# A one-core AdaLN block with routed experts: the down product as three half-precision terms

## Chip, core and metric

The kernel runs on 1 core of one Trainium2 chip. The metric is device time in microseconds (us) of one execution. The engines are named as the profile names them: PE (TensorE matmuls), PEld (its weight loads), DVE (VectorE), ACT (ScalarE), POOL (GpSimd), SP (SyncE, which issues most DMAs). "PE's queue" below is the order in which PE takes its instructions; every engine takes its own in order.

## What is computed

1024 tokens (4 batches of 256) with 256 features go through a modulated layer norm, a linear attention with a residual, a second modulated layer norm, a router that picks 2 of 8 experts for each token, and the experts. The part that the change touches is the experts:

```python
for e in range(8):
    gate = silu(xt @ Wg[e].T)                # 256 -> 704
    up = xt @ Wu[e].T                        # 256 -> 704
    out = out + gate * up @ Wd[e].T * comb[:, e:e + 1]   # 704 -> 256
```

## The kernel before

**Two parts.** The first 120 us are the front: ten steps `k = 0..9` of a software pipeline over the four batches (the attention, the second norm, the router's logits), then the routing (`routing_choice`, `routing_places`, `routing_table`), which sorts 2048 token-expert pairs into 23 tiles of 128 slots, each tile with one expert. The second part is `tile_step` for tiles 0 to 22.

**In the front** batch b is at stage `at_step(k, n)` when b = k - n. On ACT, stage 1 reads Q out of PSUM (L678) and lets PE compute the attention sums (L489) and then the attention output (L501); stage 2 turns the sums into weights (L686, L694); stage 5 copies h2T (L704), and the router's matmuls follow (L533). On DVE, stage 3 adds the attention output (L993) and stage 4 normalises (L998 to L1018). Between these stages the same queues carry the preparation of the experts' first-layer weights W1.

**Preparation of W1 for expert e** splits its float32 matrices in a high and a low f16 half under one power-of-two scale: SP loads both matrices in a staging buffer (L354; two buffers, each free again when `low` of its expert is done); ACT squares them with a running sum (`sum_squares`, L638); PE adds the sums over partitions (`norm`, L414, two matmuls of 2 columns each); DVE makes the scale (`power_scale`, L862 to L865); ACT writes the high halves (`high`, L646, four instructions of 704 columns); DVE writes the low halves (`low`, L873, four of 704). Experts 0 to 3 are prepared in the steps, 4 and 5 around the routing, 6 and 7 in tiles 1 to 6. W2 (the down matrix) is loaded in float32 and used as it is.

**A tile c** on PE: `gate_up(c)` (18 f16 matmuls: 3 terms, 2 chunks, 3 pieces; L572), `turn_slots(c+1)` (2 transposes, L561), `down(c-1)` (6 float32 products, each recorded as 2 matmuls of 256 columns; L600), `turn_act(c)` (6 transposes, L584). For c < 8, `gate_up(c)` waits until W1 of expert c is split, whatever expert the tile has. ACT makes the silu of each piece (L723), copies the next tile's rows to f16 (L717) and copies a third of the turned activations (L733, L734); DVE multiplies (L1043), makes the low half of the rows and the slot's factors (L1032 to L1037), scales the result (L1052) and copies the other two thirds (L1067). POOL scatters the result and gathers rows by indirect DMA (L1142, L1128).

## Time and profile before

| | us |
|---|---|
| three runs | 319.64, 319.98, 322.03 |
| median | 319.98 |
| the profiled execution's own time | 321.41 |
| its span, first to last instruction | 319.57 |
| mean granted TensorE clock | 0.873 of full |

Times below are in us from the start of the span. A line such as L572 is a line of the kernel. "[1.35 <-X]" behind an instruction is how long its engine sat idle before it and what ended that. In the chain of waits each piece follows from the one before it. PEclk in the table of windows is the granted share of TensorE's clock; 1.00 is 2.4 GHz and 0.50 is 1.2 GHz.

### The profile page before, as it was taken

What the parts mean: (1) busy time and instruction counts of PE and PEld (TensorE: products, weight loads), DVE (VectorE), ACT (ScalarE), POOL (GpSimd) and SP (SyncE); (2) the same over time, 40 slices, a digit from 0 to 9 for tenths busy, and PEclk for the clock granted to TensorE, in tenths of its full rate; (3) what the DMA queues carried; (4) which work ended last, traced back from release to release, by engine and by line L of the source; (5) the groups of instructions that cost most, each with busy time, mean ns of one, the idle gap of its engine ahead of it and who ended that gap; (6) DMA issues with size and microseconds to landing.
All of it is one profiled execution on the core that took longest, in us unless ns stands there. A gap on an engine that the chain in (4) does not pass through costs nothing.

```text
span 319.6 us, 4248 instructions
## 1 busy us (share of the span) xinstructions
PE 248.6 (78%) x1154; PEld 157.7 (49%) x1155; DVE 170.7 (53%) x448; ACT 119.7 (37%) x262; POOL 82.5 (26%) x93
## 2 busy tenths in 40 slices
PE   3889298967452228999997899999999999999500
PEld 0236166656352113666664466666666666666300
DVE  1356805798877972844667244444444444443236
ACT  1158367427828243564453222223232323222000
POOL 0103646531100051022242122223333222211223
PEclk9999859997555556999999799999999999999955
DMA  7993270418072925231011111011010111100083
GB/s 266 362 417 127 71 295 33 180 25 352 2 257 105 301 69 207 91 126 29 33 36 33 33 33 35 21 36 33 17 45 29 33 34 44 33 2 0 0 269 125
DMA packets 12663, 33.88 MB, mean 106 GB/s; under 512 B 2049, under 2 KB 7684, under 8 KB 11624
## 3 DMA queue, kind: packets, MB, share of 16 engines
q1 hardware_dynamic: 10152, 28.51, 24.5%
q0 software_dynamic: 2208, 5.17, 5.5%
q8 instruction: 8, 0.13, 0.2%
q10 hardware_dynamic: 288, 0.02, 0.1%
q14 instruction: 7, 0.06, 0.1%
HBM read 29.45 MB, written 5.14 MB: 108 GB/s over the span
## 4 chain that ended last, share of the span: by engine, by line
PE 68%; DVE 18%; DMA 5%; ACT 4%; issue 3%; SPq 1%; POOL 0%; DVEq 0%; POOLq 0%; ACTq 0%
PE bank L572 27%; PE bank L600 19%; PE bank L584 5%; PE bank L464 4%; PE bank L501 2%; DVE W L873 2%; ACT W L646 2%; PE bank L421 2%; DMA W<-expert_parts 2%; PE bank L477 2%; PE bank L561 2%; DMA x<-in_x 2%; PE bank L489 1%; DMA rows<-token_rows,source_i 1%; PE bank L533 1%
## 5 line engine op out<-in xcount | busy, mean ns | idle before, releaser
L572 PE MATMUL bank<-W,rows 128*128 x414 | 90.2, 374 | 4.2 <-DVE W L873 3.2
L600 PE MATMUL bank<-W,shared 128*128 (+1 forms) x276 | 67.9, 388 | 0.7 <-DVE shared L1067 0.7
L572 PEld LDWEIGHTS bank<-W,rows 128*128 128x128 f16 x414 | 41.6, 101 | 46.8 <-issue 10.4
L1043 DVE SCALAR_TENSOR_TENSOR shared<-bank,unscale,rows 128x256 f32<-128x256 f32 (+1 forms) x69 | 31.7, 461 | 60.7 <-ACT rows L723 56.2
L1142 POOL DMA_INDIRECT expert_parts<-shared,dest_i x23 | 23.3, 1014 | 131.4 <-DVE shared L1052 131.4
L600 PEld LDWEIGHTS bank<-W,shared 128*128 128x128 f32 (+1 forms) x276 | 48.7, 189 | 13.4 <-issue 8.6
L723 ACT ACTIVATE rows<-bank,unscale 128x256 f32<-128x256 f32 (+1 forms) x69 | 31.4, 455 | 51.8 <-PE bank L572 40.9
L1128 POOL DMA_INDIRECT rows<-token_rows,source_i x23 | 25.7, 1118 | 34.9 <-DVE source_i L843 28.2
L646 ACT ACTIVATE W<-staged,w_scale_bits 128x704 f16<-128x704 f32 x32 | 25.9, 870 | 11.7 <-DVE w_scale_bits L863 11.7
L733 ACT ACTIVATE shared<-bank 128x128 f32<-128x128 f32 x23 | 6.4, 277 | 62.1 <-PE bank L584 62.1
L873 DVE SCALAR_TENSOR_TENSOR W<-staged,w_scale_bits,W 128x704 f16<-128x704 f32 x32 | 29.4, 966 | 0.0
L1052 DVE TENSOR_SCALAR shared<-bank,slot_weight 128x256 f32<-128x256 f32 x23 | 11.1, 484 | 27.9 <-PE bank L600 27.9
L638 ACT ACTIVATE W<-staged 128x1408 bf16<-128x1408 f32 x16 | 21.8, 1368 | 5.3 <-DMA staged<-in_w 5.3
L584 PE MATMUL bank<-keep,shared 128*128 128x128 f32 x138 | 20.0, 281 | 1.2 <-DVE rows L1032 1.2
L584 PEld LDWEIGHTS bank<-keep,shared 128*128 128x128 f32 x138 | 14.2, 137 | 8.0 <-issue 6.6
L464 PE MATMUL bank<-W 128*128 128x512 f32 x32 | 16.8, 674 | 0.8 <-DVE gate_bias L940 0.8
L1067 DVE COPY shared<-bank 128x512 f32<-128x512 f32 x23 | 15.9, 690 | 1.3
L421 PE MATMUL bank<-W,condT 128*4 128x512 f32 x12 | 9.6, 968 | 5.4 <-ACT condT L630 5.4
L561 PE MATMUL bank<-keep,rows 128*128 128x128 f32 x46 | 9.1, 280 | 5.5 <-DMA rows<-token_rows,source_i 5.5
L489 PE MATMUL bank<-kinv,rows 128*128 128x1 f32 x32 | 4.9, 274 | 8.1 <-ACT shared L678 7.7
L477 PE MATMUL bank<-W 128*128 128x256 f32 x48 | 11.2, 382 | 0.0
L464 PEld LDWEIGHTS bank<-W 128*128 128x128 f32 x32 | 6.8, 222 | 8.2 <-issue 8.2
(155 smaller groups left out, 255.6 us busy)
## 6 DMA issues: line engine op xcount, KB each, us to landing
staged<-in_w SPq DMA_DIRECT2D x8, 1408.0 KB, 6.4
W<-in_w SPq DMA_DIRECT2D x8, 768.0 KB, 8.8
W<-expert_parts SPq DMA_DIRECT2D x8, 256.0 KB, 4.8
W<-in_wmod SPq DMA_DIRECT2D x3, 512.0 KB, 7.4
token_rows<-rows SPq DMA_DIRECT2D x1, 1040.0 KB, 5.8
x<-in_x SPq DMA_DIRECT2D x4, 256.0 KB, 8.8
W<-mod_rows SPq DMA_DIRECT2D x4, 256.0 KB, 4.4
out<-x SPq DMA_DIRECT2D x4, 256.0 KB, 2.3
```

The costliest lines, as they stand in the source:

```text
L464: mm = pe.matmul(bank[3 + t][:, :], hT[:, col:col + P], v3(w_inT, DC)[:, dc, D:3 * D], start=(dc == 0), stop=(dc == DC - 1))
L477: mm = pe.matmul(bank[bk][:, c:c + S], v3(w_inT, DC)[:, dc, w0:w0 + P], hT[:, dc * TOKENS + b * S:dc * TOKENS + (b + 1) * S], start=(dc == ...
L572: mm = pe.matmul(bank[2 + n][:, 0:2 * w], slot[:, kc * P:(kc + 1) * P], W1_pairs[:, bass.ds(e * 2 + part, 1), :, kc, n * PIECE:n * PIECE + w],
L584: mm = pe.transpose(bk[0:rows, col:col + P], act[:, fc * P:fc * P + rows], keep[:, C_ID:C_ID + P])
L600: mm = pe.matmul(bank[7][:, 0:D], actT[0:rows, fc * P:(fc + 1) * P], W2[0:rows, bass.ds(e * W2_EXP + fc * D, D)], start=(fc == 0), stop=(f ...
L638: sc.activation(W1_b16[:, at:at + W1_MAT], staged[e % STAGED][:, m * W1_MAT:(m + 1) * W1_MAT], ACT.Square, accum_out=sumsq[:, 2 * e + m:2 ...
L646: sc.activation(w1_part(e, 0, m, kc), staged[e % STAGED][:, at:at + F], ACT.Identity, scale=w_scale[:, 2 * e + m:2 * e + m + 1]).then_inc( ...
L723: sc.activation(sig[:, n * PIECE:n * PIECE + w], bank[2 + n][:, 0:w], ACT.Silu, scale=unscale[c % 2][:, 0:1]).then_inc(s["sig_ok"], 1)
L873: ve.scalar_tensor_tensor(w1_part(e, 1, m, kc), staged[e % STAGED][:, at:at + F], w_scale[:, 2 * e + m:2 * e + m + 1], w1_part(e, 0, m, kc ...
L1043: ve.scalar_tensor_tensor(act[:, n * PIECE:n * PIECE + w], bank[2 + n][:, w:2 * w], unscale[c % 2][:, 1:2], sig[:, n * PIECE:n * PIECE + w ...
L1128: po.indirect_dma_start(xs[j % 4], None, rows_d, bass.IndirectOffsetOnAxis(source_i[:, j:j + 1], 0), bounds_check=last_token, oob_is_err=F ...
L1142: po.indirect_dma_start(parts_d, bass.IndirectOffsetOnAxis(dest_i[:, j:j + 1], 0), y_sb[r], None, bounds_check=last_part, oob_is_err=False ...
```

## The change

W2 and the activations are split in high and low f16 halves as W1 and the rows are, and the down product becomes 18 f16 matmuls of 256 columns (high x high, high x low, low x high). What goes with it:

- **W2 is prepared**: per expert one unit of 1536 columns: squares with a running sum (ACT), a `norm` matmul of one column (PE), `power_scale` (DVE), `high` in two instructions of 768 columns (ACT), `low` in two of 768 (DVE; for experts 5, 6 and 7 on POOL, two instructions for each half, after the scatters of tiles 1, 4 and 6).
- **W1's scale** comes from the largest neuron's norm: the squares are written without a running sum, PE adds them up in 8 matmuls of 352 columns with bf16 ones (before: 2 of 2 columns), and `power_scale` begins with a reduction over 352 columns.
- **Staging** is by unit (one matrix), in five smaller buffers; each load waits for `low` of the unit five before it.
- **Where it stands**: the tables below name step or tile and (expert, W1 or W2).
- **Tile**: ACT writes the high half of the turned activations (512 and 256 columns), DVE subtracts for the low half (512 and 256), in place of the copies; the last chunk of the activations overlaps the one before it, so that all transposes and products have 128 rows. DVE gets one small instruction more for the slot's weight.

```diff
+        SQUARES_AT = {0: (0, W1_OF), 1: (1, W1_OF), 3: (0, W2_OF), 4: (1, W2_OF), 5: (2, W1_OF), 6: (3, W1_OF),
+                      7: (2, W2_OF), 8: (3, W2_OF), 9: (4, W1_OF)}
+        NORM_AT = {1: (0, W1_OF), 2: (1, W1_OF), 4: (0, W2_OF), 5: (1, W2_OF), 6: (2, W1_OF), 7: (3, W1_OF), 8: (2, W2_OF)}
+        HIGH_AT = {2: (0, W1_OF), 3: (1, W1_OF), 4: (0, W2_OF), 5: (1, W2_OF), 6: (2, W1_OF), 7: (3, W1_OF), 8: (2, W2_OF)}
+        LOW_AT = {3: (0, W1_OF), 4: (1, W1_OF), 5: (0, W2_OF), 6: (1, W2_OF), 7: (2, W1_OF), 8: (3, W1_OF), 9: (2, W2_OF)}
+        TILE_SQUARES = {0: [(5, W1_OF)], 1: [(5, W2_OF)], 4: [(6, W2_OF)], 6: [(7, W2_OF)]}
+        TILE_SQUARES_END = {2: [(6, W1_OF)], 4: [(7, W1_OF)]}
+        TILE_NORM = {1: [(5, W1_OF)], 2: [(5, W2_OF)], 3: [(6, W1_OF)], 5: [(6, W2_OF), (7, W1_OF)], 7: [(7, W2_OF)]}
+        TILE_HIGH = {1: [(5, 0)], 2: [(5, 2)], 3: [(6, 0)], 5: [(6, 2), (7, 0)], 7: [(7, 2)]}
+        TILE_HIGH_END = {1: [(5, 1)], 3: [(6, 1)], 5: [(7, 1)]}
+        TILE_LOW = {0: [(4, 2)], 2: [(5, 1)], 4: [(6, 1)], 6: [(7, 1)]}
+        TILE_LOW_END = {1: [(5, 0)], 3: [(6, 0)], 5: [(7, 0)]}
+        POOL_LOW = {1: [(5, 2)], 4: [(6, 2)], 6: [(7, 2)]}
...
+            def norm(e, of):
...
+                    for k in range(count):
+                        mm = pe.matmul(bank[n % 2][:, 0:FOLD], ones16[:], parts[:, k, :], start=(k == 0), stop=(k == count - 1))
...
@@ down
-                for fc in range(FC):
-                    rows = min(P, F - fc * P)
-                    mm = pe.matmul(bank[7][:, 0:D], actT[0:rows, fc * P:(fc + 1) * P],
-                                   W2[0:rows, bass.ds(e * W2_EXP + fc * D, D)],
-                                   start=(fc == 0), stop=(fc == FC - 1))
+                terms = [(a, fc, part) for a, part in ((act_hi, 0), (act_hi, 1), (act_lo, 0)) for fc in range(FC)]
+                for k, (a, fc, part) in enumerate(terms):
+                    mm = pe.matmul(bank[7][:, 0:D], a[:, fc * P:(fc + 1) * P],
+                                   W2_16[:, bass.ds(e * 2 * W2_EXP + part * W2_EXP + fc * D, D)],
+                                   start=(k == 0), stop=(k == len(terms) - 1))
...
@@ scalar, the steps (highs stands where high stood: before the read of Q)
-                if k in (2, 3, 6, 7):
-                    high({2: 0, 3: 1, 6: 2, 7: 3}[k], 0)
+                if k in HIGH_AT:
+                    highs(HIGH_AT[k], 0)
                 for b in at_step(k, 1):
                     sc.wait_ge(s["q_done"], b + 1)
...
@@ scalar, the tile, behind the silus and slots_out
+                for prep in at_tile(TILE_SQUARES, i, c):
+                    squares(*prep)
+                for unit in at_tile(TILE_HIGH, i, c):
+                    high(*unit)
+                sc.wait_ge(s["at_done"], 2 * (4 * i + c) + 1)
+                sc.activation(act_hi[:, 0:4 * P], bank[5][:], ACT.Copy).then_inc(s["act_hi_ok"], 1)
                 sc.wait_ge(s["at_done"], 2 * (4 * i + c) + 2)
+                sc.activation(act_hi[:, 4 * P:6 * P], bank[6][:, 0:2 * P], ACT.Copy).then_inc(s["act_hi_ok"], 1)
...
@@ vector, after the steps
+            power_scale(3, W2_OF)
             routing_choice(ve, link)
-            power_scale(4)
+            power_scale(4, W1_OF)
             routing_places(ve, link)
+            power_scale(4, W2_OF)
             routing_table(ve, link)
-            power_scale(5)
+            low(3, 2)
             low(4, 0)
             low(4, 1)
...
@@ gpsimd, for W2 of experts 5, 6 and 7
+                for h, cols in enumerate(halves(e, m)):
+                    po.wait_ge(s["hi_ok"], 2 * n + h + 1)
+                    klink(po.tensor_scalar(staged[n % STAGED][:, cols], staged[n % STAGED][:, cols], scale_of(e, m), None, ALU.mult))
+                    po.tensor_tensor(unit_out(W1_16, W2_16, e, m, 1)[:, cols], staged[n % STAGED][:, cols],
+                                     unit_out(W1_16, W2_16, e, m, 0)[:, cols], ALU.subtract).then_inc(s["pool_lo_ok"], 1)
```

In a step, `power_scale` stands on DVE behind the read of Q (L964, L966) and ahead of L993; PE's `norm` stands ahead of the Q product for k < 5 and behind the transposes of L524 for k >= 5; ACT's squares close a step. PE's `norm(3, W2)` follows the steps, `norm(4, W1)` and `norm(4, W2)` the counting matmuls (L545). In a tile, PE's `norm` stands between `down(c-1)` and `turn_act(c)`, DVE's `power_scale` between the result (L1052) and the activations. `down(c)` for c < 8 waits until W2 of expert c is split. ACT after the steps does the exponential, then `high` of (3, W2), (4, W1), the squares and `high` of (4, W2).

## Rows read from the trace of the kernel before

**Rows 1.** The page's first part: busy time, share, instructions of each engine

```profile
span 319.6 us, 4248 instructions
PE 248.6 (78%) x1154; PEld 157.7 (49%) x1155; DVE 170.7 (53%) x448; ACT 119.7 (37%) x262; POOL 82.5 (26%) x93
```

**Rows 2.** Windows: length, each engine's busy us (instructions), PEclk, DMA share, GB/s

```profile
71.50:82.90 11.40, 7.61 (x34) 6.06 (x34) 9.67 (x27) 9.54 (x14) 1.71 (x2) 0.65 0.61 255
82.90:94.50 11.60, 6.79 (x30) 6.51 (x30) 9.20 (x22) 4.37 (x7) 0.86 (x1) 0.50 0.40 137
94.50:120.40 25.90, 6.44 (x30) 4.32 (x29) 21.00 (x90) 13.77 (x19) 4.47 (x4) 0.50 0.51 168
120.40:177.00 56.60, 52.30 (x258) 32.17 (x258) 32.57 (x74) 27.15 (x59) 13.89 (x13) 0.95 0.22 79
177.00:237.00 60.00, 59.97 (x298) 37.70 (x298) 24.78 (x62) 16.14 (x46) 14.42 (x15) 0.97 0.10 30
```

**Rows 3.** Chain of waits, start of tiles 0, 9 and a late one: start, us, what

```profile
120.38 6.44 PE bank L572 x18
...
193.63 3.57 PE bank L572 x18
...
237.89 3.57 PE bank L572 x18
241.67 2.79 PE bank L600 x12
244.46 0.81 PE bank L584 x6
245.26 3.56 PE bank L572 x18
```

**Rows 4.** Groups by form: count | busy us, mean ns | idle before

```profile
L572 PEld LDWEIGHTS bank<-W,rows 128*128 128x128 f16 x414 | 41.6, 101 | 46.8 <-issue 10.4
L638 ACT ACTIVATE W<-staged 128x1408 bf16<-128x1408 f32 x16 | 21.8, 1368 | 5.3 <-DMA staged<-in_w 5.3
L822 DVE TENSOR_REDUCE slot_tile<-shared 128x16 f32<-128x384 f32 x1 | 0.6, 554 | 0.0
L704 ACT ACTIVATE W<-bank 128x512 f32<-128x512 f32 x4 | 2.3, 585 | 8.2 <-PE bank L533 4.4 <-PE bank L524 3.8
L1113 POOL TENSOR_TENSOR rows<-W 128x512 f32<-128x512 f32 x4 | 5.4, 1352 | 0.3
L1116 POOL TENSOR_SCALAR ksq_max<-ksq 128x2 f32<-128x2 f32 x4 | 0.9, 213 | 0.0
```

**Rows 5.** Instructions in time, ACT and DVE, steps 6 and 8: start, us

```profile
76.46 3.20 ACT L646 ACTIVATE W<-staged,w_scale_bits 128x704 f16<-128x704 f32 x4 [1.82 <-DVE w_scale_bits L863]
89.12 3.54 DVE L873 SCALAR_TENSOR_TENSOR W<-staged,w_scale_bits,W 128x704 f16<-128x704 f32 x4
```

**Rows 6.** Chain of waits, steps 4 to 6

```profile
60.97 0.48 ACT shared L678
...
62.72 1.85 PE bank L501 x8
...
70.58 0.80 DVE W L993 x2
71.52 3.52 PE bank L501 x8
```

**Rows 7.** Chain of waits, end of the steps and counting

```profile
92.63 1.89 PE bank L533 x8
94.54 0.67 DVE lg L756 x4
...
100.51 0.43 PE bank L414 x2
```

**Rows 8.** Instructions in time around the gate of tile 7

```profile
173.00 0.87 PE L584 MATMUL bank<-keep,shared 128*128 128x128 f32 x6
177.03 3.58 PE L572 MATMUL bank<-W,rows 128*128 x8 [3.16 <-DVE W L873]
```

More of the change, by code:

```diff
@@ L55 @@
 C_COLS = C_LOW + P
+W1_OF, W2_OF = 0, 1
+PREPARED = [(0, W1_OF), (1, W1_OF), (0, W2_OF), (1, W2_OF), (2, W1_OF), (3, W1_OF), (2, W2_OF), (3, W2_OF),
+            (4, W1_OF), (4, W2_OF), (5, W1_OF), (5, W2_OF), (6, W1_OF), (6, W2_OF), (7, W1_OF), (7, W2_OF)]
+UNITS = [(e, m) for e, of in PREPARED for m in ((0, 1) if of == W1_OF else (2,))]
+NTH = {prep: n for n, prep in enumerate(PREPARED)}
+UNIT = {unit: n for n, unit in enumerate(UNITS)}
+UNIT_COLS = max(W1_MAT, W2_EXP)
 S_BIN, S_BSWAP, S_BOUT = 0, 6, 7
@@ L97, in laid_out @@
     turned = [np.concatenate([by_partition(np.ascontiguousarray(m[e].T)) for m in (Wg, Wu)], axis=1) for e in range(E)]
[L98 to L99 removed]
+    gap = np.zeros((FC * P - F, D), np.float32)
+    at = (FC - 1) * P
+    down = [by_partition(np.concatenate([Wd[e].T[:at], gap, Wd[e].T[at:]], axis=0)) for e in range(E)]
     w_in_t = np.concatenate([W_in.T, W_in[:P][pairs].T], axis=1)
@@ L258, in small_col, with unit_out, halves, units_of @@
             return small[:, c:c + 1]
-        def w1_part(e, part, m, kc):
-            at = (2 * e + part) * W1_EXP + m * W1_MAT + kc * F
-            return W1_16[:, at:at + F]
+        def unit_out(buf1, buf2, e, m, part):
+            if m == 2:
+                at = (2 * e + part) * W2_EXP
+                return buf2[:, at:at + W2_EXP]
+            at = (2 * e + part) * W1_EXP + m * W1_MAT
+            return buf1[:, at:at + W1_MAT]
+        def halves(e, m):
+            w = (W2_EXP if m == 2 else W1_MAT) // 2
+            return [slice(h * w, (h + 1) * w) for h in range(2)]
+        def units_of(e, of):
+            return [(e, 0), (e, 1)] if of == W1_OF else [(e, 2)]
+        def scale_of(e, m):
+            c = 4 * e + (3 if m == 2 else 1)
+            return w_scale[:, c:c + 1]
         W1_pairs = W1_16.rearrange("p (x m c f) -> p x m c f", m=2, c=DC, f=F)
@@ L466, in _ @@
                         mm.then_inc(s["kv_done"], 1)
-                if k in (1, 2):
-                    norm(k - 1)
+                if k in NORM_AT and k < 5:
+                    norm(*NORM_AT[k])
                 for b in at_step(k, 1):
@@ L526, in _ @@
                     mm.then_inc(s["th_done"], 1)
-                if k in (6, 7):
-                    norm(k - 4)
+                if k in NORM_AT and k >= 5:
+                    norm(*NORM_AT[k])
                 for b in at_step(k, 6):
@@ L615, in tile_step @@
                     down(i, c - 1)
-                if isinstance(i, int) and i == 0 and c in NORM_TILES:
-                    norm(NORM_TILES[c])
+                for prep in at_tile(TILE_NORM, i, c):
+                    norm(*prep)
                 turn_act(i, c)
@@ new lines, in low, with lows @@
+                for h, cols in enumerate(halves(e, m)):
+                    ve.wait_ge(s["hi_ok"], 2 * n + h + 1)
+                    ve.scalar_tensor_tensor(unit_out(W1_16, W2_16, e, m, 1)[:, cols], staged[n % STAGED][:, cols], scale_of(e, m),
+                                            unit_out(W1_16, W2_16, e, m, 0)[:, cols], ALU.mult, ALU.subtract).then_inc(s["lo_ok"], 1)
+            def lows(prep, turn):
+                units = units_of(*prep)
+                for e, m in units[turn:turn + 1]:
+                    low(e, m)
@@ L1055, in tile_step @@
             def tile_step(i, c):
-                first = isinstance(i, int) and i == 0
                 mult_pieces(i, c)
@@ L1145, in _ @@
                     gather(j + 4)
+                for unit in POOL_LOW.get(j, []):
+                    low(*unit)
             po.wait_ge(s["gateb_in"], 16 * B)
```

306 lines of the change are left out of this document (172 added, 134 removed).

## The prediction

> **What bounds the kernel now.** I read the page's totals first. PE is busy for 78% of the span, but no other engine is idle enough to ignore [rows 1]. The windows then split the span. In tiles 8 to 15 PE is busy 59.97 of 60.00 us at the full clock, so PE alone sets the pace there, while DVE and ACT have more than half their time free [rows 2]. In the steps and the routing it is different. From 71.5 to 94.5 PE is busy for 14.4 of 23.0 us and DVE for 18.9, and in the routing DVE has 21.0 of 25.9 us, with TensorE at half clock [rows 2]. The chain of waits there alternates between DVE, PE and ACT [rows 6, 7]. A microsecond taken off PE is thus worth a microsecond in the tiles, and one put on ACT, DVE or PE's queue in the front costs up to its full length. The change takes from the first and puts on the second.
>
> **The gain per tile.** The chain of one late tile is 3.57 (gate and up), about 0.2 (two transposes), 2.79 (down), 0.81 (six transposes); the next tile's gate and up start 7.37 after this one's [rows 3]. The gate and up matmuls stream 3 terms x 2 chunks x 1408 columns = 8448 columns in 3.57 us, 0.423 ns a column. A down matmul in f16 has 256 columns: 0.108 us, if its weight load (101 ns [rows 4]) lies under the one before, as the loads of L572 do. 18 x 0.108 = 1.95 us in place of 2.79: 0.84, with the last chunk now at full height. I take 0.85 a tile, so a period of 6.5. From above: pairs that don't overlap would take 18 x (0.101 + 0.108) = 3.76 us.
>
> What ran beside `down` must still fit. Per tile ACT loses two copies and gets 512 and 256 columns, about 0.6 + 0.4 (585 ns for 512 [rows 4]); DVE gets about 0.7 + 0.4 in place of its copy, and one small instruction more. ACT is then busy near 2.8 and DVE near 4.1 (3.3 before) of 6.5 us (from 16.1 and 24.8 us in 60 [rows 2]). Late tiles stay bound by PE. The high and low activations are ready some 1.6 us into the next gate and up, which lasts 3.57, so `down` doesn't wait. For 23 tiles that is 19.6 us, if nothing else happened.
>
> **The preparation in the front.** Prices: a W2 unit costs ACT squares of 1536 columns, 1.37 x 1536/1408 = 1.5 us [rows 4], and `high` of 2 x 768 columns at 0.80 per 704, 1.75 us [rows 5]; `low` costs DVE 2 x 0.885 x 768/704 = 1.95 us [rows 5]; its scale 0.5 plus one dependent instruction, 0.65. The W1 `norm` streams 8 x 352 = 2816 columns: 1.2 us at full clock, 2.4 at half; before it was 0.43 at half clock [rows 7]. The new reduction over 352 columns: 554 x 352/384 = 0.5 us [rows 4]. Now place by place, as the delay it adds to the chain:
>
> - Steps 1 and 2: two reductions and the longer `norm`, some 1.5 us on DVE's chain. Part of it is taken back, because PE then starts the K and V products nearer to its return to full clock. I take 0, from above 1.5.
> - Step 4: ACT's `high(0, W2)` stands before the read of Q (L678), but its scale is made by DVE in the same step behind DVE's own read of Q. Before, ACT read Q at 60.97 [rows 6]. Now DVE reads Q (0.8), makes the scale (0.35), then ACT writes 1.75 us and only then reads Q, near 64.0: **3.0**. PE's sums and y(1) (62.72) wait for that.
> - Step 5: DVE runs `low(0, W2)` (1.95) and the scale (0.65) ahead of L993, which stood at 70.58 right behind the normalisation: 2.6. ACT again has `high(1, W2)` (1.75) ahead of the sums and weights of the last batch, so that PE's y(3) (71.52 before) waits for ACT: 1.6 more. Together **4.2**.
> - Steps 6 and 7: PE's `norm` of (2, W1) and (3, W1) at half clock, 2.4 - 0.45, and the reduction 0.5, each directly ahead of what DVE does next: **2.5 + 2.4**. `low(1, W2)` lies under y(3), 3.52 us of PE at half clock [rows 6]; without it, 1.95 more.
> - Step 8: `high(2, W2)` ahead of the last h2T copy: **1.1**.
> - Step 9: `low(2, W2)` and the scale of (3, W2) on DVE ahead of the logits (94.54 [rows 7]). 2.6, of which DVE waited about 1.4 anyway: **1.2**.
> - Routing: `norm(4, W1)` in place of 0.43 [rows 7] at half clock 2.0, reduction 0.5, one dependent multiply and a copy 0.3, the scale of (4, W2) ahead of `routing_table` 0.65: **3.4**.
> - `low(3, W2)` ahead of `low(4, ...)` fits under the first gather, less 0.2.
>
> Sum 18.0: tile 0 should start near 138.4, not 120.4.
>
> **The preparation in the tiles.** Tiles 0 to 8 took 73.25 us from the start of tile 0 (120.38) to that of tile 9 (193.63) [rows 3]; the gate of expert 7 cost about 5 of it, PE idle for 3.16 us on DVE's `low` and then slow [rows 8]. Now they are 9 x 6.5 = 58.7, and on top: half clock in tile 0, 2.9; `norm`s between `down` and `turn_act`, 3 x 1.2 + 3 x 0.3 = 4.5. In tiles 2 and 4 the second half of `high` W1 stands on ACT ahead of the next silus: 1.2 and 1.9. In tiles 3 and 6 `high` waits for a scale which DVE makes behind its own `low` and result; the activations' high half waits behind it, DVE's low half behind that, and the next `turn_slots` and `down` behind that: 2.8 and 4.2. Last, W2 of expert 7: its `high` ends about 1.5 us into tile 8 and POOL then has four instructions of 768 columns before `down(7)`, due 3.8 us into the tile. A two-input POOL instruction costs 1352 ns per 512 columns [rows 4], 2.0 us for 768. For the one-input kind there is only 213 ns for 2 columns [rows 4]; bounds 0.2 and 2.0, I take 1.3. 2 x 3.3 = 6.6, behind POOL's two DMA issues: `down(7)` waits about 5.0 (3 to 7). These sum to 22.5, so 81.2 us: **8.0 longer**. The preparation of experts 5 to 7 is 3 x 9 us of ACT, and with ACT's own 2.8 a tile it fills some 49 of 52 us, so little slack is left to absorb an order that is wrong.
>
> The Trainium skill (GPSIMD Engine Reference, Engine selection) has one-input work on POOL at about line rate and two-input work about twice as slow as on VectorE. By it the one-input instruction would be an estimated 0.9 us and the wait some 0.8 us shorter; no row here shows it.
>
> **The sum.** 319.6 + 18.0 + 8.0 - 14 x 0.85 (tiles 9 to 22, 11.9) = 333.7 us of span. The profiled execution's own time is 321.41 and its span 319.57; the median of the runs is 319.98, 0.4 above the span. So I forecast 334.
>
> **Rivals.**
>
> - *The preparation hides* (faster). If ACT and DVE ran the W2 units in their idle stretches, only `norm` and reductions would remain (about 8 in the front) and tiles 0 to 8 would not lose: 319.6 + 8 - 19.6 + 0 to 4, near 310. For it: over the span ACT is busy 37% and DVE 53% [rows 1]. Against it: engines take their queues in order, and steps 4 and 5 have the scale behind the read on DVE and `high` ahead of the read on ACT. It decides if front and tiles 0 to 8 together add less than 11.9. Chance 0.06.
> - *Half of it hides* (within 1%): the front adds 8 and tiles 0 to 8 add 4, so 320. This needs PE at full clock through steps 6 to 9, against the windows' 0.50 to 0.65 [rows 2]. Chance 0.05.
> - *More is lost*: POOL slower than 2 us an instruction under DVE's traffic, a half-clock stretch after each stall (the gate of tile 7 cost one: eight matmuls of L572 took 3.58 there, and usually eighteen do [rows 3, 8]), steps 1 and 2 in full: 334 + 3 + 4 + 1.5, beyond 343. Chance 0.07.
> - *The loads don't hide at 256 columns*: 3.76 - 2.79 = 0.97 more a tile in place of 0.85 less, 23 x 1.82 = 42 us above the forecast, 376. Against it: the same loads hide wholly under L572's matmuls, where 18 x (101 ns + the matmuls' columns) would be 5.4 us, not 3.57 [rows 3, 4]. Chance 0.02. The Trainium skill (TensorE: Matmul & The Clock Gate, "The mechanism" of Part 3) says LDWEIGHTS overlaps matmuls in flight only if the row group differs. By that rule full-height loads wouldn't overlap; the trace disagrees with it for 512 columns.
> - The forecast: 0.80.
>
> **Range and chances.** Low: steps 6 to 9 and the routing at full clock (-4), POOL's short price (-2), a stall or two in tiles 3 and 6 absorbed (-3): 325. High: 343 as above. The cases below 325 hold 0.11 and those above 343 0.09, so 325 to 343 leaves out 2 in 10. A measurement of this kernel tells about 1% from no change. Faster by over 1%: 0.06; within 1%: 0.05; slower: 0.89.
>
> **What would show it.** After: the late tiles' gate and up start 6.5 us apart and the 18 down matmuls take 1.95; if 3.8, the loads don't hide. ACT's read of Q (L678's successor) for batch 3 comes about 3 us after PE's Q product ends, with ACT's idle time before it released by DVE's scale. PE idles about 4 us ahead of y(3). The bf16 `norm` takes 2.4 us at half clock in steps 6 and 7. Tile 0 starts 14 to 20 us later than 120.4; if it starts within 10, the queue argument is wrong. PE idles once for about 5 us ahead of `down(7)`, released by POOL. If the end is early although all of these show, the tiles' stalls were counted twice.

## The result, and the profile after

The changed kernel takes 344.87 us (median of four, 343.43 to 346.44) against 319.85 for the kernel before (319.64 to 322.03): a ratio of 1.077, 95% interval 1.070 to 1.084. It is slower by 25 us; the forecast was 14 slower, 334 (325 to 343), so the median lies 1.9 above the range. Timed again beside the later experiments the changed kernel took 343.01 (339.52 to 345.44), ratio 1.066 (1.059 to 1.073), which is the upper end of the range. The profile of that second run ("the changed kernel again") has a span of 341.2 us and is the one that I compare experiments with. Its code is the same.

The page's first part for the kernel after, to be read against [rows 1]:

```profile
span 344.6 us, 4994 instructions
PE 247.2 (72%) x1356; PEld 160.9 (47%) x1357; DVE 202.5 (59%) x548; ACT 151.4 (44%) x278; POOL 105.0 (30%) x105
```

PE is busy for as long as before: `down` takes some 19 us less (an estimate, 23 tiles of 0.82), and the longer norms and stretches at half clock take that up again. DVE and ACT are busy for 32 us more each, and the span grew by 25 us in which PE is idle. Line numbers from here on are those of the changed kernel: gate and up is L629, `down` L656, `turn_act` L641, the W1 `norm` L468, `high` L707, DVE's `low` L957, POOL's `low` L1241 and L1242, the read of Q L745, the attention sums L545 with ACT's weights L761, y L557.

Windows of the kernel after: length, busy us (instructions) of PE, PEld, DVE, ACT, POOL, granted clock, DMA share, GB/s. They are y(3) to the logits, the routing with the first gather, tiles 0 to 8, and 60 us of late tiles:

```profile
82.10:112.50 30.40, 18.57 (x80) 14.94 (x80) 23.07 (x58) 19.78 (x24) 2.56 (x3) 0.61 0.39 126
112.50:142.10 29.60, 8.48 (x34) 4.85 (x35) 23.62 (x97) 10.76 (x14) 4.95 (x4) 0.50 0.33 100
142.10:231.00 88.90, 72.43 (x409) 43.43 (x410) 50.79 (x127) 47.34 (x84) 38.67 (x28) 0.86 0.25 83
240.00:300.00 60.00, 60.00 (x414) 41.46 (x412) 34.47 (x93) 23.81 (x57) 18.86 (x19) 1.00 0.13 39
```

Before, the stretches that answer to the first two rows took 23.0 and 25.9 us [rows 2]. The third is where the forecast failed: tiles 0 to 8 took 73.25 us before [rows 3], they were forecast at 81.2 and take 88.9, with PE at 0.86 of its clock and idle for 16 us. The last row is the gain, with PE never idle at the full clock. A late tile in the chain of waits (start, us, what):

```profile
237.86 3.56 PE bank L629 x18
241.43 0.22 PE bank L618 x2
241.65 1.97 PE bank L656 x18
243.61 0.66 PE bank L641 x6
244.27 3.56 PE bank L629 x18
```

Eighteen down matmuls take 1.97 us (1.95 forecast) where twelve took 2.79 [rows 3], and the period is 6.40 us.

Where the rest went, by starting times in the two traces:

| start of | before | forecast | changed, again | miss |
|---|---|---|---|---|
| first z (step 3) | 54.9 | 54.9 | 54.9 | 0 |
| second z (behind step 4) | 64.6 | +3.0 | 70.2, +5.6 | 2.6 |
| y(3) (behind step 5) | 71.5 | +7.2 | 81.2, +9.7 | 2.5 |
| fourth z (step 6) | 76.5 | +9.7 | 88.2, +11.7 | 2.0 |
| x2 of batch 3 (step 7) | 84.0 | +12.1 | 97.9, +13.9 | 1.8 |
| logits (step 9) | 94.5 | +14.4 | 110.6, +16.1 | 1.7 |
| tile 0 | 120.4 | +18.0 | 140.3, +19.9 | 1.9 |
| tile 9 | 193.6 | +26.0 | 227.8, +34.2 | 8.2 |
| end | 319.6 | +14.1 | 341.2, +21.6 | 7.5 |

In the first profile tile 0 came at 142.1 and tiles 0 to 8 took 88.9; in this one 140.3 and 87.5.

### The profile page after: what moved, and what is told of

Its sections match the earlier page's. It is cut to its first block, busy times and chain, and to the rows that moved or that the text cites. A ratio compares the mean times of both kernels' runs of the same rounds, so it can differ in the third digit from the quotient of the medians.

```text
span 344.6 us, 4994 instructions
## 1 busy us (share of the span) xinstructions
PE 247.2 (72%) x1356; PEld 160.9 (47%) x1357; DVE 202.5 (59%) x548; ACT 151.4 (44%) x278; POOL 105.0 (30%) x105
## 4 chain that ended last, share of the span: by engine, by line
PE 52%; DVE 22%; ACT 8%; DMA 7%; issue 5%; SPq 3%; POOL 3%; DVEq 0%; ACTq 0%; POOLq 0%
PE bank L629 20%; PE bank L656 13%; DVE W L957 5%; ACT W L707 4%; PE bank L641 3%; DMA staged<-in_w 3%; PE bank L468 3%; PE bank L557 3%; PE bank L520 2%; PE bank L533 2%; DMA W<-expert_parts 2%; DVE shared L1165 1%; PE bank L545 1%; PE bank L618 1%; POOL staged L1241 1%
## 5 line engine op out<-in xcount | busy, mean ns | idle before, releaser
L629 PE MATMUL bank<-W,rows 128*128 x414 | 90.4, 375 | 3.9 <-DVE W L957 2.8
L629 PEld LDWEIGHTS bank<-W,rows 128*128 128x128 f16 x414 | 41.5, 100 | 47.1 <-issue 11.0
L707 ACT ACTIVATE W<-staged,w_scale_bits 128x704 f16<-128x704 f32 (+1 forms) x48 | 40.0, 889 | 50.0 <-DVE w_scale_bits L944 50.0
L656 PE MATMUL bank<-W,shared 128*128 x414 | 53.7, 283 | 10.0 <-POOL W L1242 6.5
L656 PEld LDWEIGHTS bank<-W,shared 128*128 128x128 f16 x414 | 40.9, 100 | 19.3 <-issue 12.0
L957 DVE SCALAR_TENSOR_TENSOR W<-staged,w_scale_bits,W 128x704 f16<-128x704 f32 (+1 forms) x42 | 41.0, 1024 | 0.0
L1165 DVE TENSOR_TENSOR shared<-bank,shared 128x512 f16<-128x512 f32 (+1 forms) x46 | 23.5, 552 | 19.0 <-ACT shared L799 19.0
L799 ACT ACTIVATE shared<-bank 128x512 f16<-128x512 f32 x23 | 13.6, 592 | 40.9 <-PE bank L641 40.9
L699 ACT ACTIVATE W<-staged 128x1408 bf16<-128x1408 f32 x16 | 21.2, 1369 | 4.5 <-DMA staged<-in_w 4.5
L641 PE MATMUL bank<-keep,shared 128*128 128x128 f32 x138 | 19.6, 280 | 2.9 <-DVE rows L1125 2.9
L1150 DVE TENSOR_SCALAR shared<-bank,slot_weight 128x256 f32<-128x256 f32 x23 | 11.1, 483 | 14.1 <-PE bank L656 12.5
L641 PEld LDWEIGHTS bank<-keep,shared 128*128 128x128 f32 x138 | 16.4, 146 | 3.8 <-DVE shared L1140 3.4
L468 PE MATMUL bank<-W,ones 128*128 128x352 bf16 x64 | 14.8, 391 | 2.7 <-ACT W L699 2.7
L557 PE MATMUL bank<-shared,W 128*128 128x256 f32 x32 | 11.5, 521 | 4.1 <-ACT W L761 4.1
L1241 POOL TENSOR_SCALAR staged<-staged,w_scale_bits 128x768 f32<-128x768 f32 x6 | 13.9, 2319 | 0.1
L1221 POOL TENSOR_TENSOR rstd<-var_eps,half_neg 128x2 f32<-128x2 f32 x4 | 3.4, 861 | 32.4 <-DVE var_eps L975 32.4
```

Source lines behind the costliest of these rows:

```text
L468: mm = pe.matmul(bank[n % 2][:, 0:FOLD], ones16[:], parts[:, k, :], start=(k == 0), stop=(k == count - 1))
L629: mm = pe.matmul(bank[2 + n][:, 0:2 * w], slot[:, kc * P:(kc + 1) * P], W1_pairs[:, bass.ds(e * 2 + part, 1), :, kc, n * PIECE:n * PIECE + w],
L641: mm = pe.transpose(bk[:, col:col + P], act[:, at:at + P], keep[:, C_ID:C_ID + P])
L656: mm = pe.matmul(bank[7][:, 0:D], a[:, fc * P:(fc + 1) * P], W2_16[:, bass.ds(e * 2 * W2_EXP + part * W2_EXP + fc * D, D)], start=(k == 0) ...
L707: sc.activation(unit_out(W1_16, W2_16, e, m, 0)[:, cols], staged[n % STAGED][:, cols], ACT.Identity, scale=scale_of(e, m)).then_inc(s["hi_ ...
L957: ve.scalar_tensor_tensor(unit_out(W1_16, W2_16, e, m, 1)[:, cols], staged[n % STAGED][:, cols], scale_of(e, m), unit_out(W1_16, W2_16, e, ...
```

## The stalls in the changed kernel

PE in time, kernel after (start, us, what, idle before it): the sums and y(1) of step 4, y(3) of step 6, then tile 3's `down` and norm, tile 7's gate and up, tile 8's `down` and transposes.

```profile
65.59 1.84 PE L545 MATMUL bank<-kinv,rows 128*128 128x1 f32 x8 [3.57 <-ACT shared L745]
67.28 3.76 PE L557 MATMUL bank<-shared,W 128*128 128x256 f32 x8
...
82.08 3.78 PE L557 MATMUL bank<-shared,W 128*128 128x256 f32 x8 [4.13 <-ACT W L761]
...
172.28 3.26 PE L656 MATMUL bank<-W,shared 128*128 x18 [0.47 <-issue]
175.34 2.18 PE L468 MATMUL bank<-W,ones 128*128 128x352 bf16 x8
...
206.55 5.98 PE L629 MATMUL bank<-W,rows 128*128 x18 [2.77 <-DVE W L957]
...
225.90 4.02 PE L656 MATMUL bank<-W,shared 128*128 x18 [6.45 <-POOL W L1242]
229.71 1.48 PE L641 MATMUL bank<-keep,shared 128*128 128x128 f32 x6
```

ACT in time, same kernel, steps 4 and 5:

```profile
63.21 1.76 ACT L707 ACTIVATE W<-staged,w_scale_bits 128x768 f16<-128x768 f32 x2 [2.74 <-DVE w_scale_bits L944]
...
79.27 1.76 ACT L707 ACTIVATE W<-staged,w_scale_bits 128x768 f16<-128x768 f32 x2 [9.24 <-DVE w_scale_bits L944]
```

The waits are the forecast ones, in the forecast places: `high` stood waiting 2.74 us for DVE's scale with the read of Q behind it, PE waited 3.57 us for that read, y(3) 4.13 us for ACT, `down(7)` 6.45 us for POOL. What was not in the sum stands in the second column, the durations. y(1), eight matmuls that had taken 1.85 us before [rows 6], takes 3.76 behind its stall; `down` in tile 8 takes 4.02 where 1.97 is usual; tile 7's gate and up 5.98 where 3.56 is (5.42 in the second profile, and 5.42 in the kernel before, which has a stall there too). Behind these stalls the granted clock is 0.50 for some microseconds (windows 65.6 to 71.0, 82.1 to 86.0, 206.55 to 209.0 and 225.9 to 229.9). It isn't so behind every one: in tile 6 the six transposes behind 1.72 us of idle time take their usual 0.84, at a granted clock of 1.00. The profile tells nothing yet of whether the half clock costs time or only fills waits, so it was tried.

## The experiments

Two theories run through them. *Q*: an engine takes its queue in order, so W2's preparation costs what stands ahead of the next thing that the attention or the tile needs. *W*: ACT, DVE and PE have more to do and no room for it, wherever it stands. The experiments ran in four groups. The kernel before, timed beside each group, had medians of 319.8 to 321.5 us, so a difference of under 2 us between kernels of two groups is not clear.

### Only `high` of W2 behind the reads of steps 4 and 5

```diff
 # ACT, ahead of the read of Q
-                if k in HIGH_AT:
+                if k in HIGH_AT and k not in (4, 5):
                     highs(HIGH_AT[k], 0)
 # ACT, behind the sums and their weights
-                    highs(HIGH_AT[k], 1)
+                    highs(HIGH_AT[k], 0 if k in (4, 5) else 1)
```

> Only ACT's order in steps 4 and 5 is changed: `high(0, W2)` and `high(1, W2)` stand behind the attention sums and their weights, no longer ahead of the read of Q. The work is the same. Theory Q (an engine takes its queue in order, so what counts is what stands ahead of the attention's next read): the read of Q for batch 3 comes back from 64.9 to about 61.7 us, PE's y(3) waits for ACT 1.8 us less, and tile 0 starts 4.5 us earlier (3 to 6): about 340.4 us. Theory W (ACT, DVE and PE simply have more to do in the front, wherever it stands): tile 0 starts where it did, 344.9 us within 1.

334.45 us (333.83 to 335.32); tile 0 at 131.9 in place of 140.3. This much of the loss is one of order, but the gain of 8.4 to 8.6 us is nearly twice the 4.5 of theory Q. PE in time of this kernel:

```profile
60.65 1.02 PE L545 MATMUL bank<-kinv,rows 128*128 128x1 f32 x8 [0.77 <-ACT shared L745]
61.53 1.97 PE L557 MATMUL bank<-shared,W 128*128 128x256 f32 x8
...
73.02 3.57 PE L557 MATMUL bank<-shared,W 128*128 128x256 f32 x8 [2.04 <-DVE W L1084]
```

The wait fell from 3.57 to 0.77, and the sums and y(1) behind it from 1.84 + 3.76 to 1.02 + 1.97: another 2.6 us that come with the wait. The first z, ahead of the edit, came 1.2 us earlier already (53.7 for 54.9; profiles of one and the same front differ by as much). So 7.2 of tile 0's 8.4 us are the edit's, and 4.5 and 2.6 make 7.1.

### PE kept busy through its waits

In the tiles, with every wait left as it is:

```diff
+        BUSY = {(3, 1): (15, 11), (6, 3): (15, 15), (7, 0): (24, 15), (8, 2): (56, 15)}
...
+                for _ in range(count):
+                    pe.matmul(bank[0][:, 0:D], W2_16[:, 0:P], W2_16[:, 0:D], start=True, stop=True)
```

> The same kernel, with f16 matmuls of 256 columns into an unused bank put where PE stood idle in the tiles: 15 ahead of the slots of tile 3, 15 ahead of the transposes of tile 6, 24 ahead of the gate product of tile 7, 56 ahead of `down(7)`, at about 0.11 us each the length of each idle stretch. Their results are used by nothing. Theory H (half clock behind each stall costs about 7 us in tiles 3, 7 and 8: 2.1 + 2.4 + 2.7): those stretches run at full clock and the time falls by 5.5 us (3 to 7.5): 339.4. Theory S (the stalls are set by ACT, DVE and POOL, and a faster PE only waits longer at the next one): no change, within 1 us. If filling costs more than the idle time holds, the time rises by up to 2 us.

336.87 us (336.76 to 338.06). Its tile 0 came at 140.3 as in the changed kernel again, so the two traces compare directly: tile 3 10.39 in place of 11.92, tile 7 6.59 in place of 8.28, tile 8 13.32 in place of 15.61, tile 9 6.40 in place of 6.71; tile 6 stayed at 12.79, so its filler changed nothing. Together 5.8 us, and theory S is out. PE in time, tiles 6 to 8 of this kernel (L671 are the added matmuls):

```profile
196.74 1.80 PE L671 MATMUL bank<-W 128*128 128x256 f16 x15
...
199.43 2.78 PE L671 MATMUL bank<-W 128*128 128x256 f16 x24
202.37 3.74 PE L631 MATMUL bank<-W,rows 128*128 x18 [0.15 <-issue]
...
212.86 6.28 PE L671 MATMUL bank<-W 128*128 128x256 f16 x56
219.47 2.31 PE L658 MATMUL bank<-W,shared 128*128 x18 [0.34 <-POOL W L1255]
```

The gate product waits just as long for DVE and `down(7)` for POOL as before, but both then run at the full clock (1.00 from 199.4 to 206.0 and from 212.8 to 221.8). Matmuls whose results nobody reads make the kernel 6 us faster. Tile 7's part of it, 1.7 us, is one that the kernel before left lying as well: its tile 7 takes 9.07 us, a late tile 7.38.

In the front, the same in steps 4 to 6 (30, 20 and 34 such matmuls ahead of the sums, the transposes and y(3)):

```diff
+                if k == 4:
+                    keep_busy(30, bank[1], 2)
                 for b in at_step(k, 2):
...
+                if k == 6:
+                    keep_busy(34, bank[0], 3)
                 for b in at_step(k, 3):
...
+                if k == 5:
+                    keep_busy(20, bank[1], 2)
                 for b in at_step(k, 5):
```

> The changed kernel with f16 matmuls of 256 columns into an unused bank in three idle stretches of PE in the front: 30 ahead of the attention sums of step 4 (3.57 us idle), 20 ahead of the transposes of step 5 (2.51), 34 ahead of y(3) in step 6 (4.13). Nothing uses their results; all waits stay. Theory H (a part of what e1 gave back beyond the 4.5 us forecast is TensorE's clock: behind these stalls y(1) took 3.76 us where it took 1.85 before): y(1) and its sums give back 2.6, y(3), its transposes and the norm of step 6 3: 5 us less (3 to 6), about 339 against 344. Theory O (e1's gain is all order: DVE and ACT set the front, a faster PE waits longer): no change within 1.5 us.

338.12 us (337.52 to 340.00) against 343.01 (339.52 to 345.44): 4.9 less in the medians, though the two ranges overlap by 0.5. Tile 0 came at 135.0 in place of 140.3; 1.1 of these 5.3 us stood already at the first z, ahead of the added matmuls. PE in time, this kernel:

```profile
59.77 3.44 PE L476 MATMUL bank<-W 128*128 128x256 f16 x30
63.52 1.02 PE L552 MATMUL bank<-kinv,rows 128*128 128x1 f32 x8 [0.30 <-ACT shared L756]
64.40 1.97 PE L566 MATMUL bank<-shared,W 128*128 128x256 f32 x8
...
77.42 1.99 PE L566 MATMUL bank<-shared,W 128*128 128x256 f32 x8 [0.40 <-ACT W L772]
```

The sums and y(1) are back at 1.02 + 1.97 with the wait still there, and y(3) went from 3.78 to 1.99. Some 4 to 5 us of the front's loss can be had back by the clock alone, with the order left as it is. Before, y(3) took 3.52 at half clock too [rows 6]: a part of this gain is one that the kernel before left lying as well.

### W1's scale from sums as before, W2's preparation whole

```diff
-                        ins = sc.activation(w, staged[n % STAGED][:, 0:W1_MAT], ACT.Square)
+                    ins = sc.activation(w, staged[n % STAGED][:, 0:W2_EXP if m == 2 else W1_MAT], ACT.Square,
+                                        accum_out=sumsq[:, 3 * e + m:3 * e + m + 1])
...
-                        mm = pe.matmul(bank[n % 2][:, 0:FOLD], ones16[:], parts[:, k, :], start=(k == 0), stop=(k == count - 1))
+                        mm = pe.matmul(bank[n % 2][:, 0:1], keep[:, C_ONE:C_ONE + P], sumsq[:, 3 * e + m:3 * e + m + 1],
+                                       start=(m == 0), stop=(m == 1))
...
-                    link(ve.tensor_reduce(norm_sq[:, 0:1], bank[n % 2][:, 0:FOLD], AX.X, ALU.max))
```

> Only W1's scale is made as in the kernel before: ACT's squares sum themselves, `norm` is two one-column matmuls in place of eight of 352 columns, and DVE's reduction over 352 columns is gone. W2's preparation stays whole. Theory Q: steps 1 and 2 give back 1.5, steps 6 and 7 2.4 and 2.0, the routing 2.5, tiles 1, 3 and 5 together 4 (the norms and their half-clock part): about 12 us less, 333 (330 to 337). If the norms hide behind other work: less than 3 us. If W2's squares, `high` and `low` alone carry the loss: no change.

334.62 us (333.43 to 335.09): 8.4 under the changed kernel again and 10.3 under its first timing, where 12 were forecast. Tile 0 came 8.4 us earlier (131.9), tiles 0 to 8 took 85.3 in place of 87.5. The norms by the neurons, which are no part of the f16 product itself, cost more than a third of the whole loss. In the tiles they were partly covered: 2 us, not 4.

### W2's low halves on DVE in place of POOL

```diff
-        TILE_LOW = {0: [(4, 2)], 2: [(5, 1)], 4: [(6, 1)], 6: [(7, 1)]}
-        TILE_LOW_END = {1: [(5, 0)], 3: [(6, 0)], 5: [(7, 0)]}
-        POOL_LOW = {1: [(5, 2)], 4: [(6, 2)], 6: [(7, 2)]}
+        TILE_LOW = {0: [(4, 2)], 2: [(5, 1)], 3: [(5, 2)], 4: [(6, 1)], 6: [(7, 1)]}
+        TILE_LOW_END = {1: [(5, 0)], 3: [(6, 0)], 5: [(6, 2), (7, 0)], 7: [(7, 2)]}
+        POOL_LOW = {}
```

> Only the low halves of W2 of experts 5, 6 and 7 move from POOL to DVE (after tile 3's scales, at the ends of tiles 5 and 7). Theory P (POOL's four instructions of 768 columns are what `down(7)` waited 6.45 us for, and its two-input ones hold DVE up in tiles 4 to 6): the wait ahead of `down(7)` falls to 1 us or less, the half clock behind it (2.7 us) goes too, and of the stall and the slow gate product in tile 7 about half goes: 9 us less, 336 (332 to 339). Theory D (DVE has no room in tiles 3 to 8: 1.95 us more in each of three tiles comes back as waits of the slots and activations): 3 us less or nothing, 342 to 346.

335.46 us (334.79 to 335.88), 7.5 to 9.4 less. PE in time, tiles 7 and 8 of this kernel:

```profile
202.88 6.39 PE L627 MATMUL bank<-W,rows 128*128 x18 [2.04 <-DVE W L955]
...
217.63 2.46 PE L654 MATMUL bank<-W,shared 128*128 x18 [1.45 <-DVE W L955]
```

Tile 8 fell from 15.61 to 8.47 us: 5.0 of that is the wait (6.45 to 1.45) and the rest the clock behind it. That part held. The other did not: the stall ahead of tile 7's gate was 2.04 where it had been 2.77, its product still ran at half clock (6.39), and tiles 6 and 7 took 21.2 where they had taken 21.1. Taking POOL's work away did not help there. Whether POOL had no part in that stall, or DVE's own 1.95 us a unit cost as much in its place, this experiment doesn't tell.

### The same work in another order

In the tiles, with `high` of steps 4 and 5 as in the first experiment: the units stand in the order in which they are due, a `high` one turn behind its norm, one unit on ACT ahead of the activations' copies and one behind them, all low halves on DVE.

```diff
-            (4, W1_OF), (4, W2_OF), (5, W1_OF), (5, W2_OF), (6, W1_OF), (6, W2_OF), (7, W1_OF), (7, W2_OF)]
+            (4, W1_OF), (4, W2_OF), (5, W1_OF), (6, W1_OF), (5, W2_OF), (7, W1_OF), (6, W2_OF), (7, W2_OF)]
...
+        TILE_ACT = {0: [(5, 0, 's'), (5, 1, 's')], 1: [(6, 1, 's'), (5, 2, 's')], 2: [(5, 1, 'h')], 3: [(6, 1, 'h'), (7, 0, 's')],
+                    4: [(5, 2, 'h')], 5: [(7, 1, 'h')], 6: [(6, 2, 'h')], 7: [(7, 2, 'h')]}
+        TILE_ACT_END = {0: [(6, 0, 's')], 1: [(5, 0, 'h')], 2: [(6, 0, 'h')], 3: [(7, 1, 's')], 4: [(7, 0, 'h')], 5: [(6, 2, 's')], 6: [(7, 2, 's')]}
+        TILE_NORM = {1: [(5, W1_OF)], 2: [(6, W1_OF)], 3: [(5, W2_OF)], 4: [(7, W1_OF)]}
+        TILE_NORM_EARLY = {6: [(6, W2_OF)], 7: [(7, W2_OF)]}
```

> The edit of e1_high_after_reads, and another order of the preparation in the tiles, with the same work: the experts' units stand in the order in which they are due (5 and 6 of W1, 5 of W2, 7 of W1, 6 and 7 of W2), ACT makes a `high` one turn after the norm that it needs, about one unit between its slots' copy and its activations' copies and one behind them, and DVE makes all low halves, W2's too. Theory Q (the stalls of tiles 3, 6, 7 and 8 are waits for scales, for `high` and for POOL, not lack of time on ACT or DVE): tiles 0 to 8 take 67 us in place of 87 to 89, so some 20 less than e1: 315 (311 to 320). Theory W (ACT and DVE have no room: DVE has about 57 us of work in them): tiles 0 to 8 stay over 78 us, 326 or more.

314.88 us (314.48 to 316.55): 1.8% under the kernel before, ratio 0.982 (0.973 to 0.992), with all of the change's work in it. Window of this kernel over its tiles 0 to 8, to be read against the third window above:

```profile
133.50:199.80 66.30, 63.69 (x409) 41.47 (x410) 51.39 (x134) 47.79 (x84) 15.11 (x14) 0.97 0.33 111
```

DVE does 51.39 us of work in 66.3 where it did 50.79 in 88.9, ACT 47.79 where it did 47.34. The work is the same and there was room for it: 21 to 23 us were waits, half clock and, on DVE, instructions that POOL made longer (last section). ACT's waits for a scale, by the table of waits, the kernel after first and this kernel second:

```profile
ACT W L707 <- DVE w_scale_bits L944: 50.0, 12, 9.2
```

```profile
ACT W L707 <- DVE w_scale_bits L945: 30.9, 8, 7.0
```

In the front, more of the same on top (ACT's `high` of steps 6 to 8 behind the h2T copy; DVE's scales and lows of steps 5 to 9 between the second norm's differences and h2; expert 4's norms and scales behind the routing table):

```diff
 # DVE, behind the differences
+                if k in NORM_AT and k >= 5:
+                    power_scale(*NORM_AT[k])
...
 # ACT
                     sc.activation(h2T, bank[2][:], ACT.Copy).then_inc(s["h2T_ok"], 1)
+                if k in HIGH_AT and k >= 6:
+                    highs(HIGH_AT[k], 0)
+                    highs(HIGH_AT[k], 1)
...
 # DVE, routing
-            power_scale(4, W1_OF)
             routing_places(ve, link)
-            power_scale(4, W2_OF)
             routing_table(ve, link)
+            power_scale(4, W1_OF)
             low(3, 2)
+            power_scale(4, W2_OF)
```

> e5 and, in the front, more moved behind what the attention needs, with the same work: ACT's `high` of steps 6 to 8 behind the h2T copy, DVE's scales and lows of steps 5 to 9 behind the second norm's differences, the scales and norms of expert 4 behind the routing's table, under the first gather. Theory Q: steps 6 to 9 give back about 4 and the routing 2.5: 6 us less than e5 (3 to 9), about 309. Theory W (half-clock PE and DVE's sheer length set steps 6 to 9, whatever the order): within 2 us of e5.

314.08 us (313.36 to 314.56): 0.8 less, not 6. The fourth z came 4.7 us earlier (76.7 against 81.4) and x2 of batch 3 6.1 earlier (84.9 against 91.0), but h2T of batch 3 0.9 later (100.8 against 99.9). DVE in time of this kernel shows where it was given back:

```profile
92.60 3.54 DVE L961 SCALAR_TENSOR_TENSOR W<-staged,w_scale_bits,W 128x704 f16<-128x704 f32 x4
...
96.05 0.88 DVE L1117 SCALAR_TENSOR_TENSOR rows<-W,rstd 128x256 f32<-128x256 f32 x2
```

The lows now stood ahead of h2's rows of batch 3 (L1117), behind a scale whose `norm` ended at 91.6. I had moved them from one place ahead of the chain to another. With W1's sums as well:

> e6 and the edit of e2_w1_sum (W1's scale from ACT's own sums, no eight-matmul norm and no reduction). If what e2 took away (10.2 us) is the path's own length and not a part of the stalls that e5 and e6 removed, it comes off again: PE's three norms in the tiles 3.6, steps 1 to 7 about 4, so 7 to 8 us less than e6, about 301. If the two overlap: 3 us or less.

307.43 us (306.99 to 310.78), 6.7 less than without: the length of the norms is a cost of its own, beside the stalls. Then the lows one place further, behind h2:

```diff
                     ins.then_inc(s["h2_ok"], 1)
+                if k in NORM_AT and k >= 5:
+                    power_scale(*NORM_AT[k])
+                if k in LOW_AT:
+                    if k >= 5:
+                        lows(LOW_AT[k], 0)
+                    lows(LOW_AT[k], 1)
```

> e7 with DVE's scales and lows of steps 5 to 9 one place further back, behind the rows of h2, and PE's norms of these steps behind the router's product. In e6 they stood between the differences and h2, and h2T of batch 3 came at 100.8 us, 16 us behind x2 of batch 3 (84.8). Theory Q: h2T of batch 3 comes some 8 us behind x2 in place of 15, the logits then wait for 9 us of lows on DVE, so tile 0 starts 3 us earlier than e7's 126.8: 304 (302 to 307). Theory W (DVE's total length from x2 to the logits decides): no change, 307.4.

304.89 us (304.56 to 305.69), ratio to the kernel before 0.953 (0.950 to 0.956). DVE in time, this kernel:

```profile
85.35 0.88 DVE L1102 SCALAR_TENSOR_TENSOR rows<-W,rstd 128x256 f32<-128x256 f32 x2 [0.18 <-POOL rstd L1222]
...
88.03 3.54 DVE L952 SCALAR_TENSOR_TENSOR W<-staged,w_scale_bits,W 128x704 f16<-128x704 f32 x4
```

h2's rows come at 85.35, h2T of batch 3 at 92.5 (10 us behind x2, where 8 were expected, and 16 in e6), the logits at 100.1 and tile 0 at 125.0. This is the fastest kernel of the study, 4.7% under the one before. It has W2 and the activations in halves as the change has them, but W1's scale again from sums.

### W2's preparation left out

```diff
-PREPARED = [(0, W1_OF), (1, W1_OF), (0, W2_OF), (1, W2_OF), (2, W1_OF), (3, W1_OF), (2, W2_OF), (3, W2_OF),
-            (4, W1_OF), (4, W2_OF), (5, W1_OF), (5, W2_OF), (6, W1_OF), (6, W2_OF), (7, W1_OF), (7, W2_OF)]
+PREPARED = [(e, W1_OF) for e in range(E)]
...
+                sp.dma_start(v3(W2[:, e * W2_EXP:(e + 1) * W2_EXP], 4),
+                             keep_d[:, 0:3 * P].rearrange("p (a n) -> p a n", a=1).to_broadcast([P, 4, 3 * P])
+                             ).then_inc(w2_in[e], 16)
```

> The whole preparation of W2 is left out (no squares, norm, scale, high or low of W2): its halves are plain transfers of constants, so the output is not the reference's. All else is the changed kernel, `down` with it. This prices the preparation. Theory Q: the front loses 15 us of its added 21.7 (steps 4 and 5 12, steps 8 and 9 2.3, routing 0.7) and tiles 0 to 8 come to about 68 us, 21 less: 309 (304 to 315), so the products alone would be a gain of 11 over the kernel before. Theory R (the front's loss is mostly W1's new norm): 330 or more.

This kernel leaves out W2's values: its halves are constants, and the products are all there. 311.45 us (310.68 to 313.11). W2's preparation thus costs the changed kernel 343.0 - 311.5 = 31.5 us. In the order of e6 the same preparation, in full, ends at 314.1, only 2.6 us above this kernel, so most of the 31.5 is order. But 2.6 is less than what the preparation costs in e6, since this kernel keeps the changed kernel's order of W1's units: its tile 6 takes 9.9 us and its tiles 0 to 8 take 69.4, where e6's take 65.8 with all of W2's work. In the front, where tile 0 comes at 126.8 here and at 132.2 in e6, the preparation still costs 5.4. What W2's preparation costs beside W1's best order was not tried.

### The changed kernel again

> The changed kernel once more, unedited, beside e9 and e10. Its front took 139.5 and 140.3 us up to tile 0 in two experiments that left the front alone, and 142.1 in its own profile; here it should be 139 to 142, and the time 342 to 345.

343.01 us, tile 0 at 140.3. Of the first profile's extra 1.8 us in the front, 0.9 stand at the first z already, behind a half-clock stretch from 23.4 to 26.8 that no other profile of this front shows. The rest comes in step 6, where the transposes and the norm behind y(3) are longer at half clock (the norm takes 1.80 for 1.36).

### One unit on POOL, with time to spare

```diff
-        TILE_LOW_END = {2: [(5, 1)], 3: [(6, 1)], 4: [(5, 2)], 5: [(7, 1)], 6: [(6, 2)], 7: [(7, 2)]}
-        POOL_LOW = {}
+        TILE_LOW_END = {2: [(5, 1)], 3: [(6, 1)], 5: [(7, 1)], 6: [(6, 2)], 7: [(7, 2)]}
+        POOL_LOW = {3: [(5, 2)]}
```

> e10 with one unit, the low half of W2 of expert 5, back on POOL, in tile 4, where it has over 8 us until `down(5)` in tile 6. So POOL's length (7.7 us a unit) can delay nothing by itself, and what is left is what POOL does to DVE beside it. In the changed kernel's trace DVE's 128 x 1 instruction took 0.94 us in place of 0.21 and its `low` of W1 3.77 us in place of 1.81 while POOL's two-input instructions ran. Theory L (POOL costs only through its own length): the time stays within 1 us of 304.9 or falls, since DVE has 1.95 us less to do, and DVE's instructions in tiles 4 and 5 keep their lengths. Theory S (DVE stands still beside POOL's two-input instructions, some 1.6 us each): DVE instructions that meet them grow by up to 1.6 us, 2 of them, and the time does not fall; tiles 4 and 5 together take the same or up to 2 us more than e10's 14.2.

306.80 us (305.84 to 309.25) against e10's 304.89: no gain. Whether it is a loss of 1.9 stays open: the ratios to the kernel before, 0.957 (0.952 to 0.963) and 0.953 (0.950 to 0.956), overlap, and of the 3.8 us between the two profiles 2.3 stand at tile 0 already, ahead of the edit. What the traces show is how long single instructions take. POOL in time of this kernel, then DVE in time beside it:

```profile
166.35 2.22 POOL L1243 TENSOR_SCALAR staged<-staged,w_scale_bits 128x768 f32<-128x768 f32 x1
168.66 1.65 POOL L1244 TENSOR_TENSOR W<-staged,W 128x768 f16<-128x768 f32 x1
170.28 2.21 POOL L1243 TENSOR_SCALAR staged<-staged,w_scale_bits 128x768 f32<-128x768 f32 x1
```

```profile
168.78 1.54 DVE L1127 SCALAR_TENSOR_TENSOR slot_weight<-rows,second 128x1 f32<-128x1 f32 x1
...
171.12 1.80 DVE L953 SCALAR_TENSOR_TENSOR W<-staged,w_scale_bits,W 128x704 f16<-128x704 f32 x2
```

A DVE instruction of one column, 0.21 us everywhere else, began 0.12 us into POOL's two-input instruction and ended with it, 1.54 us later. Beside POOL's one-input instruction DVE's `low` kept its 1.80 for two, but the next instruction of one column took 0.73 for 0.22. Tiles 4 and 5 took 13.75 us in place of 14.17 and tile 6 8.14 in place of 6.54, so tiles 0 to 8 are 1.7 us longer, a tile later than theory S had it. That a part of this is the transfers that POOL issued late behind its `low` was not tried apart.

## Why the prediction was right or wrong, step by step

**Right.** That it is slower, and how: PE's gain in the tiles against a longer front and stalls. Gain per tile: period 6.40 against 6.5 forecast; tiles 9 to the end gave back 12.5 us, not 11.9. The loads hide at 256 columns too. One sentence of the Trainium skill (TensorE: Matmul & The Clock Gate, "The mechanism" of Part 3) has them overlap only where the row group differs; here, at full height, 18 matmuls with 18 loads of some 0.10 us take 1.97, so the trace disagrees. An earlier sentence of the same section lets a load into the background weight buffer go ahead of the matmuls in flight as well; the trace fits that one. The front's places, one by one from the table: step 5 +4.1 (4.2 forecast), step 6 +2.0 (2.5), step 7 +2.2 (2.4), steps 8 and 9 together +2.2 (2.3), routing and gather +3.8 (3.6 with `low(3, W2)`), steps 1 and 2 nothing (0). One condition of the terms failed without much effect: step 6's norm ran at full clock (1.36 us in the second profile), only step 7's took the 2.4 of half clock (2.53). That the order is what costs in steps 4 and 5 and in the tiles is shown by e1 and e5. In steps 6 to 9 and the routing another order gave only 0.8 (e6) before the norms were shortened and the lows went last (e10).

**Wrong: step 4's term, 3.0.** It measured 5.6. I summed what stands ahead of ACT's read of Q and let PE go on at its old clock. The read itself came at 63.95 in the second profile, forecast near 64.0, 3.0 later than before; so the queue's part was right. But PE idled 3.57 us for that read, and the sums and y(1) behind it then took 2.6 us longer; e9 took just that away and left the wait.

**Wrong: tiles 0 to 8, +8.0.** They measured +14.2 (87.5 against 73.25). The clock behind the stalls was in no term of the sum, only in the rival "more is lost", at 4 us; e4 measures 5.8 for it, 5.5 of them in tiles 3, 7 and 8. Two terms were too small. POOL's `low(7, W2)`, with `down(7)` waiting 5.0: it waited 6.45, since a one-input POOL instruction of 768 columns takes 2.2 us (1.3 taken, bounds 0.2 and 2.0) and the two-input one 1.64 (2.0 taken), 7.7 a unit for 6.6. The Trainium skill (GPSIMD Engine Reference, Engine selection), by which one-input work runs at about line rate, made it an estimated 0.9; here it is slower than the two-input one. And tile 6, which had 6.5 and a stall of 4.2, took 12.8, 2.1 more. DVE's two `low` of W1 take 3.77 us for 1.81 there, beside POOL's instructions, which no term had; that they are the cause was not tried apart. These three are 9.1. Tile 0, with 2.9 for half clock, gave back 2.1 (7.3 us for 9.4), and the shorter period (6.40 for 6.5) some 0.9.

Some readings and sums were slightly off, with no effect on the outcome: 9 x 6.5 is 58.5 and not 58.7, the window with PE busy 59.97 us covers tiles 7 to 14, and DVE had 3.0 us a late tile before and not 3.3.

**The rivals.** "More is lost" is what happened, just above its bound of 343, with its clock part twice as large as I had it (some 2.6 in step 4 and 5.8 in the tiles against 4) and its POOL part half as large (1.5 against 3). That the total still came within 2 us of the range owes something to luck: tile 0 and the period gave back 3 us of what was missed. I had [rows 8] in hand: the eight matmuls at 3.58 us behind a stall of 3.16. I charged that stretch to the kernel before and then, in the sum, to none of the five stalls that I forecast for the kernel after; a chance of 0.07 for a price that one row showed was too small. (Since that stretch is in the kernel before too, not all of the 5.8 is what the change costs; it was missing from the sum all the same, which was built up tile by tile.) "The preparation hides" is false for the change as it is and true for the same work in another order: e5 and e6 end at 315 and 314, near its 310, though tile 0 still comes 12 to 13 us later than before. The argument that ACT's 49 of 52 us leave no room was weak: ACT does its 47.8 us in e5's 66.3.

## To carry to other kernels

Preparation that shares queues with a dependent chain costs by where it stands: a write that waits for a scale, placed ahead of the chain's next read, costs the wait as well as its own length; put it one turn behind what it needs, in the order of due times. When a sum forecasts that PE stands still, look for a row that shows what PE does behind a stall of that length, and if that is at half clock, add a term for it. Moving work pays where it goes behind the last thing that the chain needs from that engine (e10); between two of them it merely changed which one waits (e6).
